# Causal attention in a six-stage decoder kernel: the division of the probabilities by their row sums moved from GpSimd to VectorE

## The reference

```
q = (x @ Wq).reshape(b, t, HKV, G, HD)      # HKV = 4, G = 4, HD = 64, t = 512
k = (x @ Wk).reshape(b, t, HKV, HD)
v = (x @ Wv).reshape(b, t, HKV, HD)
scores = jnp.einsum('bqhgd,bkhd->bhgqk', q, k) / jnp.sqrt(jnp.float32(HD))
scores = jnp.where(causal, scores, NEG)
attn = jax.nn.softmax(scores, axis=-1)
ctx = jnp.einsum('bhgqk,bkhd->bqhgd', attn, v).reshape(b, t, HQ * HD)
return ctx @ Wo
```

## Time and profile before

| | |
|---|---|
| time, median of 3 runs | 1184.0 us (1183.9 to 1187.14) |
| the profiled execution, own time | 1186.93 us |
| its span in the profile | 1185.2 us |
| causal attention, its scores to its last output projection | 596 to 937 us of the span |
| busy share of the span | PE 81%, DVE 67%, ACT 53%, POOL 30% |

### The profile page before, as it was taken

One profiled execution on the slowest core, in us unless ns is written; L12 is line 12 of the kernel. 1 busy time (PEld: TensorE's weight loads), 2 busy tenths in 40 slices (PEclk: granted clock), 3 DMA queues, 4 the chain that ended last, 5 costly groups with the idle time before them and its releaser, 6 DMA issues. The chain is left out here.

```text
span 1185.2 us, 20933 instructions
## 1 busy us (share of the span) xinstructions
PE 962.1 (81%) x6175; PEld 495.7 (42%) x6175; DVE 793.7 (67%) x1693; ACT 626.2 (53%) x1548; POOL 355.7 (30%) x533
## 2 busy tenths in 40 slices
PE   4489999999999736899799999999999677352870
PEld 2122233333333134566545555555555435331760
DVE  8789999999999286566556665666656689243111
ACT  4548888888888702222365656656566233110540
POOL 4212222222222131000244454545545423225004
PEclk9759999999999956799899999999999889766995
DMA  1000000000000000000100000000000100105762
GB/s 45 1 1 1 1 2 2 0 0 0 0 0 0 1 15 14 6 16 20 35 14 8 12 10 7 13 7 13 7 8 1 32 0 1 54 1 155 204 188 71
DMA packets 47723, 28.63 MB, mean 24 GB/s; under 512 B 12152, under 2 KB 44208, under 8 KB 47664
## 3 DMA queue, kind: packets, MB, share of 16 engines
q1 hardware_dynamic: 46640, 25.81, 7.9%
q0 software_dynamic: 1024, 2.10, 0.6%
HBM read 22.79 MB, written 5.11 MB: 24 GB/s over the span
## 5 line engine op out<-in xcount | busy, mean ns | idle before, releaser
L509 DVE TENSOR_REDUCE a_nmax<-a_rows 128x2 f32<-128x1024 f32 x256 | 299.2, 1218 | 14.6 <-PE a_rows L415 11.4
L552 ACT ACTIVATE a_probs<-a_turned 128x512 f32<-128x512 f32 x512 | 269.2, 603 | 40.7 <-PE a_turned L437 39.1
L1116 POOL TENSOR_TENSOR a_prob<-a_prob,a_rinv 128x256 f32<-128x256 f32 (+3 forms) x128 | 159.7, 1253 | 173.1 <-DVE a_rinv L1306 172.8
L1299 DVE TENSOR_REDUCE a_nmax<-a_score 128x2 f32<-128x256 f32 (+3 forms) x128 | 105.6, 825 | 124.2 <-PE a_score L1155 119.8
L1253 ACT ACTIVATE a_prob<-a_score,a_nmax 128x128 f32<-128x128 f32 (+3 forms) x256 | 132.7, 523 | 82.4 <-DVE a_nmax L1299 82.0
L437 PE MATMUL a_turned<-a_q,a_qk 32*128 32x512 bf16 x512 | 137.4, 391 | 7.6 <-ACT a_probs L552 5.6
L400 PE MATMUL a_acc<-a_probs,a_vg 128*32 128x512 f32 x1024 | 139.0, 615 | 0.8 <-ACT a_probs L552 0.7
L415 PE MATMUL a_rows<-a_qk 32*128 32x512 bf16 x512 | 111.9, 401 | 13.2 <-DVE a_nmax L509 6.2
L1152 PE MATMUL a_score<-a_k_s,a_q_s 64*128 64x384 f32 (+3 forms) x512 | 103.7, 481 | 2.2 <-ACT a_prob L1253 1.3
L437 PEld LDWEIGHTS a_turned<-a_q,a_qk 32*128 32x128 bf16 x512 | 35.3, 91 | 155.1 <-ACT a_probs L552 131.8
L1312 DVE COPY a_pt<-a_turn 128x128 f32<-128x128 f32 (+3 forms) x224 | 92.2, 447 | 1.4 <-PE a_turn L1166 1.4
(11 more groups left out here) (288 smaller groups left out, 1518.9 us busy)
## 6 DMA issues: line engine op xcount, KB each, us to landing
m_w<-L_ffn_w SPq DMA_DIRECT2D x46, 256.0 KB, 3.6
a_wq<-L_attn_Wq SPq DMA_DIRECT2D x16, 128.0 KB, 2.2
xs_sorted<-m_zeros SPq DMA_DIRECT2D x1, 1472.0 KB, 6.6
m_xs<-xs_sorted SPq DMA_DIRECT2D x5, 256.0 KB, 3.6
ys_sorted<-m_ysb SPq DMA_DIRECT2D x5, 256.0 KB, 3.3
g_X<-x SPq DMA_DIRECT2D x4, 256.0 KB, 3.6
m_wgu<-L_ffn_gate_up_proj SPq DMA_DIRECT2D x8, 128.0 KB, 2.1
a_wk<-L_attn_Wk SPq DMA_DIRECT2D x32, 32.0 KB, 2.0
```

Source lines behind the costliest of these rows:

```text
L509: dve.tensor_reduce(nmax[i % 2][:, p // 2, (p % 2) * 2:(p % 2) * 2 + 2], rows[n % 2][:, :, :], AX_X, ALU.max, negate=True).then_inc(row_ou ...
L552: act.activation(probs[:, (tb % 2) * 4 + j, :], turned[n % 3][:, :], ACT.Exp, scale=float(HD0) ** -0.5).then_inc(turn_out, 1)
L1116: pool.tensor_tensor(pr, pr, spread(rinv[:, t % RING, :], 2, width), ALU.mult).then_inc(scl, 1)
L1299: dve.tensor_reduce(nmax[:, t % RING, :], score[t % 2][:, :, 0:width], AX_X, ALU.max, negate=True).then_inc(mx, 1)
```

## The change

GpSimd's division goes; VectorE does it right behind the reciprocal of the same item, one `tensor_scalar` for each head with the head's column of `rinv` as a scalar per partition. VectorE first waits on its own semaphore `ri` for the reciprocal to have been written.

```
@@ GpSimd @@
                     pool.tensor_copy(v_s[i % 2][:, :, :], vals[:, i + 2 * r, :, :]).then_inc(vcp, 1)
-                    for it in range(ITEMS):
-                        t, width = ITEMS * i + it, (BLOCKS[it % SB] + 1) * P
-                        pr = prob[t % RING][:, :, 0:width]
-                        pool.wait_ge(ri, t + 1 + 2 * ITEMS * r)
-                        pool.tensor_tensor(pr, pr, spread(rinv[:, t % RING, :], 2, width), ALU.mult).then_inc(scl, 1)
@@ VectorE, invert @@
                 dve.reciprocal(rinv[:, t % RING, :], rsum[:, t % RING, :]).then_inc(ri, 1)
+                dve.wait_ge(ri, t + 1 + 2 * ITEMS * r)
+                width = (BLOCKS[it % SB] + 1) * P
+                for j in range(2):
+                    pr = prob[t % RING][:, j, 0:width]
+                    last = dve.tensor_scalar(pr, pr, rinv[:, t % RING, j:j + 1], None, ALU.mult)
+                last.then_inc(scl, 1)
```

## The result

The changed kernel takes 1214.53 us (median of 4 runs, 1211.3 to 1220.25) against 1183.95 us (4 runs), a ratio of 1.0271 with a 95% interval of 1.021 to 1.0333. That is 30.6 us more; the forecast was +27, 1211 us.

A forecast was written before the change was run, and what follows sets the result against it. TensorE (PE) was taken to set the pace, with GpSimd off the path. Stalls of 0.70 + 0.27 + 0.70 = 1.67 us a unit over 16 units give +27 on 1184.0, so 1211 us; range 1204 to 1224.

The forecast's parts named there:

- Hidden: Rival: VectorE's idle 123 us absorbs the added 95, time stays at 1184 us, perhaps 1.5 us given back; 3 in 100.
- The slack of 0.23 us at step 0: Start of a unit: the first 256-wide copy lands 0.23 us before PE's 384-wide transposes, after a 0.04 hand-over.
- long stalls: Twice a unit, PE's 384-wide transposes wait for copies behind VectorE's 512-wide division: 0.70 us each.
- short stalls: Once a unit, PE's second 128-wide transpose waits for a 512-wide copy delayed by the 256-wide division: 0.27 us.
- The price of a division: One VectorE tensor_scalar per head: 293, 356, 418 and 481 ns for widths 128 to 512, fixed part 230.
- double rate: VectorE's tensor_scalar in SBUF handles about two elements a cycle, 0.49 ns an element; forecast case, 83 in 100.
- The held instruction: Earlier trace: a line 128 tensor_scalar took 2490 ns instead of 340 beside a GpSimd memset, taken as a rate clue.
- The wait on the own semaphore: VectorE, reciprocal to division: division starts 0.15 + 0.04 us behind the reciprocal's start, 0.12 more per item than before.
- Steps 0 to 1, 2 to 3 and 4 to 5: Places in a unit where PE was to wait: 0.70, 0.27 and 0.70 us, 1.67 a unit, none elsewhere.
- Single rate: Rival: VectorE divides one element a cycle, 335 to 731 ns by width, +46 us, 1230 us; 8 in 100.
- GpSimd's copy: Rival: GpSimd's remaining 0.40 us copy holds a division, +6.4 us, 1217; counter-argument: VectorE then waits for scores; 6 in 100.
- first unit and last items cancel: Stage's ends: last items gain under 1 us, first unit loses cover for its steps; set against each other at nothing.

The follow-up runs named there:

- e6: Changed kernel with no division on any engine, probabilities unnormalised, reciprocal releasing the transposes: 1184.06 us, ratio 0.9981 to the kernel before.
- e1: Changed kernel with the copies of item t-3 put in front of reciprocal and divisions on VectorE: 1186.69 us, ratio 1.0016 to the kernel before.
- e2: Changed kernel with one dearer, single-rate tensor_tensor for both heads in place of two tensor_scalar, same place: 1233.43 us, ratio 1.0421 to the kernel before.
- e5: Changed kernel with one single-rate tensor_tensor for both heads and the copies in front of reciprocal and division: 1189.86 us, ratio 1.0025 to the kernel before.
- e3: Changed kernel with the 512-wide items divided by GpSimd, the three narrower widths by VectorE: 1191.28 us, ratio 1.0058 to the kernel before.
- e4: Changed kernel with only the 512-wide items divided by VectorE, the others by GpSimd: 1210.43 us, ratio 1.0219 to the kernel before.

## Why the prediction was right

- **What bounds the kernel.** PE, with GpSimd off the path: shown by e6. That PE's 100% busy row hides no room was argued from the order of time; the equal 21.12 us in before, e1 and e6 bear it out, but no run made PE's own work shorter. The 1.5 us that the *Hidden* rival might have given back were not there: without any division the stage was 0.2 us shorter (e6).
- **The slack of 0.23 us at step 0.** The stall came out as addition less slack, as e2 shows with a second dose (0.345 dearer, 0.34 longer). The slack was in fact smaller. The prediction took 0.04 for the hand-over from VectorE's copy to PE, from a row of the other direction. In the changed kernel the first copy ends at 617.45 and the transposes start at 617.59; to the nanosecond it is 0.146 to 0.147 us at all 32 long stalls, 0.10 more than taken. At the 16 short stalls it is 0.056, 0.02 more than taken; there the second transpose starts 0.27 us late, as forecast, and the matmul itself then takes 0.33 us in place of 0.27. So the three stalls came out 0.10, 0.05 and 0.10 larger, 4 us in sixteen units, and this is nearly the whole miss: +27 forecast, +31 by PE's rows, +30.6 measured. Why the hand-over has two lengths is open.
- **The price of a division.** Forecast 293, 356, 418 and 481 ns, measured 284, 350, 418 and 483. The slope is 199 ns for 384 elements, 0.52 an element: the double rate. The held instruction of the earlier trace rows had pointed to it, but it was the weaker clue: in e5 it is GpSimd's `v_s` copy that takes 0.58 to 0.89 us in place of 0.40, beside a division that runs at the single rate, so meeting GpSimd does not by itself tell the rate. The Trainium skill's figure ("VectorE: DVE Perf Modes", section "The perf-mode tier table") gave an estimate of 427 ns for 512, 56 under the measurement; on the rate the trace agrees with it.
- **The wait on the own semaphore.** Reciprocal at 616.04, division at 616.23: 0.15 and a gap of 0.04, as taken. The Trainium skill ("VectorE: DVE Perf Modes", section "The DRAIN you can't avoid") says that "the semaphore costs nothing extra here", of copies that each increment one. These rows show another thing for an instruction that waits for the one before it: a gap of 0.04 in place of an overlap of some 0.08.
- **Where the stalls are.** Steps 0 to 1, 2 to 3 and 4 to 5, with 0.80, 0.32 and 0.80 us against 0.70, 0.27 and 0.70 in the working. No others appeared in the steady part. e3 and e4 separate them by width.
- **The rivals.** *Hidden*: VectorE did have the room on average, and e1 and e5 use it, but with another order. *Single rate*: made in e2, it gives 1233 us, where the rival had said 1230. The closeness is in part chance, since e2 has one instruction for both heads, with 0.12 + 1.15 added at step 0 where the rival had 1.43. *GpSimd's copy*: in the changed kernel it never ran beside a division (at 625.45, in unit 1, VectorE is idle), so it did not cost; the 512-wide divisions average 483 ns and the longest of all 256 is 489. The mechanism of this rival is real all the same: in e3 the copy did meet a division and held it. What spared the forecast is the moment of the copy, as the rival's own counter-argument had it. The clock stayed at 1.00.

Taken without a row: that first unit and last items cancel. They do, but with the signs the other way round, which is luck. The stage has grown by 31.9 us. The fourteen middle units grew by 1.99 each. The first, which was to lose more, lost 1.4; the stretch from the last unit's first scores on, which was to gain, lost 2.6.

## What to carry to other kernels

Room on an engine, as a share of its time, says nothing about what may be put in front of a hand-over on it. Look at the tightest step, find the instruction there that another engine waits for, and measure how long before its deadline it lands; what is put ahead of it costs the excess over that slack, and what was put behind it here cost 2 to 3 us in all, nearly nothing in the middle units (0.2 us a unit with VectorE busy 90%, in e5). When the profile names a releaser, first look whether it worked on the item that the waiting instruction needs. If another instruction ends next to it on the same engine, change their order: it is one edit, it changes no work, and here it returned all but 2 to 3 of 30.6 us.

## What the runs showed of the hardware

- In e3 a VectorE `tensor_scalar` from SBUF to SBUF in fp32 did not finish beside a GpSimd `tensor_tensor` or copy that was running when it started: each of a pair ended 0.08 us after the GpSimd instruction beside it, and took 0.46 and 0.42 us where 0.28 is the mean in the changed kernel. It also went the other way: a GpSimd copy of 0.40 us took 0.58 to 0.89 when it started while a VectorE `tensor_tensor` was running (e5). And the one that started first was not held: in e1 fourteen 384-wide divisions still ran when GpSimd's copy started, and took 413 to 416 ns, no more than the others.
- The time from the end of a VectorE copy to PE's next transpose was 0.147 us at the 32 long stalls of the changed kernel and 0.056 at the 16 short ones, against 0.03 from the end of PE's matmuls (a modelled end) to VectorE's reduction. A chain that goes back and forth between the two pays it each time.
